# Head squares added on POOL, layer-norm products in rounded parts, and another order of the steps

## The reference, cut to what matters

```python
for i in range(6):
    x = attn_layer(shift_tokens(x), Wqkv[i], q_scale[i], k_scale[i], Wo[i]) + x
    x = ffn_layer(shift_tokens(x), ln_g[i], ln_b[i], W1[i], b1[i], W2[i], b2[i]) + x
# attn_layer: 16 heads of 64; q and k are divided by their norm (l2norm), scaled, rotated;
# windows of 32 tokens see themselves and the window before; softmax; @ Wo
# ffn_layer:
mu = x.mean(-1); var = ((x - mu) ** 2).mean(-1)
xn = (x - mu) / sqrt(var + 1e-05) * g + bln
a, gate = split(xn @ W1 + b1); out = a * gelu(gate) @ W2 + b2
```

## Time and profile before

| | us |
|---|---|
| median of 3 runs | 1853.37 |
| lowest and highest | 1852.04, 1864.84 |
| the profiled execution's own time | 1851.59 |
| its span, first to last instruction | 1849.8 |
| PE busy | 1652.6 (89%) |
| DVE busy | 1239.1 (67%) |
| ACT busy | 1137.9 (62%) |
| POOL busy | 1000.0 (54%) |
| mean granted TensorE clock | 0.962 of full |

### The profile page before, as it was taken

How to read it: one execution, slowest core, us unless ns; L and a number is a source line. 1 busy time by engine, 2 the same in 40 slices (tenths; PEclk the granted TensorE clock), 3 DMA queues, 4 the chain that set the end, 5 groups by cost and what they waited for, 6 DMA issues and landing times.

```text
span 1849.8 us, 80254 instructions
## 1 busy us (share of the span) xinstructions
PE 1652.6 (89%) x35760; PEld 1362.8 (74%) x35760; DVE 1239.1 (67%) x1939; ACT 1137.9 (62%) x2113; POOL 1000.0 (54%) x756
## 2 busy tenths in 40 slices
PE   6458999998999999999999999999999989999986
PEld 5246787777777787778777778778777777778775
DVE  6756766765766775676676677677667667677562
ACT  2024766766666676576676666676666666667653
POOL 1025655664654575565475565476556476556441
PEclk9769999999999999999999999999999999999996
DMA  3047666556646657656656664666665665665650
GB/s 104 1 119 188 135 139 155 124 136 176 162 110 143 155 120 186 148 134 139 155 123 162 155 158 116 144 153 170 155 145 118 151 153 120 150 152 126 140 125 24
DMA packets 98441, 252.92 MB, mean 137 GB/s; under 512 B 30000, under 2 KB 36272, under 8 KB 97328
## 3 DMA queue, kind: packets, MB, share of 16 engines
q1 hardware_dynamic: 98096, 247.80, 56.2%
HBM read 44.26 MB, written 2.10 MB: 25 GB/s over the span
## 4 chain that ended last, share of the span: by engine, by line
PE 53%; DVE 14%; SPq 11%; issue 10%; ACT 8%; DMA 3%; POOL 1%; ACTq 0%; POOLq 0%; DVEq 0%
PE ps L355 48%; SPq L305 6%; SPq L316 6%; DVE E L783 4%; PE ps L542 3%; DMA Qtb<-Qtb 3%; DVE UV L722 2%; DVE rs L793 2%; ACT zs L852 2%; ACT E L852 2%; ACT PT L852 1%; DVE Kt L766 1%; ACT sq L852 1%; PE ps L497 1%; ACT Vs L852 1%
## 5 line engine op out<-in xcount | busy, mean ns | idle before, releaser
L722 DVE SCALAR_TENSOR_TENSOR UV<-ps,veca,rope 128x512 f32<-128x512 f32 x768 | 526.8, 744 | 192.3 <-PE ps L355 182.8
L1081 POOL TENSOR_TENSOR Kt<-UV 128x512 f32<-128x512 f32 x192 | 240.9, 1276 | 472.2 <-DVE UV L722 472.1
L852 ACT ACTIVATE sq<-ps 128x512 f32<-128x512 f32 (+1 forms) x400 | 231.7, 580 | 313.3 <-PE ps L355 299.5
L1081 POOL TENSOR_TENSOR Qtb<-UV 128x512 f32<-128x512 f32 x192 | 242.7, 1286 | 118.5 <-DVE UV L722 118.5
L1091 POOL TENSOR_TENSOR E<-E,mx 128x1024 f32<-128x1024 f32 x96 | 182.6, 1902 | 147.0 <-DVE mx L789 147.0
L355 PE MATMUL ps<-xh,wh 128*128 128x256 f32 x768 | 240.9, 314 | 7.1 <-ACT sq L852 4.3
L355 PE MATMUL ps<-xh,wl 128*128 128x256 f32 x768 | 221.7, 289 | 2.8 <-issue 2.8
L355 PE MATMUL ps<-xl,wh 128*128 128x256 f32 x768 | 221.5, 288 | 1.6 <-issue 1.6
L355 PEld LDWEIGHTS ps<-PT,V 64*64 64x64 f32 x12288 | 198.4, 136 | 31.5 <-issue 19.5
L355 PE MATMUL ps<-Kb,Qtb 64*32 64x64 f32 (+1 forms) x12288 | 190.0, 224 | 34.6 <-issue 34.4
L355 PE MATMUL ps<-PT,V 64*64 64x32 f32 x12288 | 215.5, 221 | 1.6 <-ACT PT L852 0.7
(11 more groups left out here) (131 smaller groups left out, 3347.1 us busy)
## 6 DMA issues: line engine op xcount, KB each, us to landing
V<-Vs SPq DMA_DIRECT2D x672, 128.0 KB
Kb<-Kt SPq DMA_DIRECT2D x384, 128.0 KB
Qtb<-Qtb SPq DMA_DIRECT2D x384, 128.0 KB, 2.4
rope<-in_c_rope SPq DMA_DIRECT2D x48, 512.0 KB
raw<-in_Wqkv SPq DMA_DIRECT2D x6, 1536.0 KB, 6.9
V<-Vs SPq DMA_DIRECT2D x96, 64.0 KB
V<-V SPq DMA_DIRECT2D x96, 64.0 KB, 2.0
wo<-in_Wo SPq DMA_DIRECT2D x6, 512.0 KB, 5.4
```

The source lines that it names most:

```text
L722: e.scalar_tensor_tensor(UV[:, p % 2, slot, :].rearrange("p (i t) -> p i t", i=2), ps[:, half, :].rearrange("p (i t) -> p i t", i=2), veca ...
L852: return e.activation(out, in_, f, **kw)
L1081: e.tensor_tensor(dst, u, v, op).then_inc(s["rot_done"], 1)
```

## The change

Three things change.

1. POOL gets a step a_sum: it adds the squares of the second halves onto those of the first. a_norm then multiplies only once per quarter instead of twice.
2. c_mu and c_var each become two F32R products. For c_mu, ACT rounds zs into the high part za[0], POOL subtracts to get the low part za[1] (c_zal). For c_var, ACT writes the square twice, once plain and once rounded, and POOL makes the remainder (c_zql). cen and mean are rounded once in the preamble.
3. The order of the list is another one.

```diff
+SCHEDULE = """b_lnq b_rcq a_vs0 c_xs c_xb a_vs1 a_v0 w_h0 a_mx0 c_zal w_l0 a_sqy0 c_zsq c_wo b_rq a_sqx0 c_zql a_my0 a_v1
+    a_sqy1 c_rs b_s0 a_x0 a_y0 c_mu a_rot0 b_sub0 b_rqt a_halo b_s1 a_sum0 c_var a_x1 a_sqx1 b_exp0 a_y1 b_scale0
+    b_s2 b_max0 b_s3 a_mx1 c_zl a_x2 b_nrm0 c_zh w_h1 a_y2 b_sub1 a_sqy2 a_my1 a_rl a_lnk a_norm0 b_pto0 c_zn
+    b_sum0 a_rot1 c_h0 b_scale1 b_max1 b_pt0 b_nrm1 a_rh b_exp1 a_rck a_mx2 a_my2 a_sqx2 a_rot2 b_sum1 b_pto1
+    c_gelu0 a_kn0 a_xs+1 b_pt1 b_att0 b_oto0 a_sp0 a_rot3 a_sp1 c_hm0 c_gelu1 b_att1 a_x3 c_h1 a_sum1 a_y3 a_sqy3
+    a_kn1 a_mx3 b_pt2 b_pto2 c_hm1 a_sqx3 b_wo a_xh+1 c_h2 a_my3 w_h2 b_att2 c_gelu2 a_xl+1 c_hm2 b_xb b_pto3
+    b_pt3 b_oto1 c_down c_fin w_l2 w_l1 c_wh c_wl b_att3 a_norm1""".split()
...
             def a_norm(m, side):
-                e.wait_ge(s["sq_done"], m * 8 + 4 * side + 4)
+                e.wait_ge(s["sqs_done"], m * 2 + side + 1)
...
-                for half in range(2):
-                    for q in range(HQ):
-                        ins = mm(ps[q * W:(q + 1) * W, NORM, side * T:(side + 1) * T], ind[:, :],
-                                 sq[:, q // 2, half, q % 2 * T:(q % 2 + 1) * T], half == 0, half == 1,
-                                 tile_position=(0, q * W))
+                for q in range(HQ):
+                    ins = mm(ps[q * W:(q + 1) * W, NORM, side * T:(side + 1) * T], ind[:, :],
+                             sq[:, q // 2, 0, q % 2 * T:(q % 2 + 1) * T], tile_position=(0, q * W))
...
             def c_mu(j, _):
-                e.wait_ge(s["z_act"], j * 2 + 2)
-                mm(ps[:, WO, 0:T], cen[:, :], zs[:, :]).then_inc(s["mu_done"], 1)
+                e.wait_ge(s["zal_done"], j + 1)
+                mm(ps[:, WO, 0:T], cen[:, :], za[:, 0, :], True, False)
+                mm(ps[:, WO, 0:T], cen[:, :], za[:, 1, :], False, True).then_inc(s["mu_done"], 1)
             def c_var(j, _):
-                e.wait_ge(s["zsq_done"], j + 1)
-                mm(ps[:, WO, T:2 * T], mean[:, :], zq[:, :]).then_inc(s["var_done"], 1)
+                e.wait_ge(s["zql_done"], j + 1)
+                mm(ps[:, WO, T:2 * T], mean[:, :], za[:, 0, :], True, False)
+                mm(ps[:, WO, T:2 * T], mean[:, :], za[:, 1, :], False, True).then_inc(s["var_done"], 1)
...
@@ ACT, c_xs and c_zsq
+                if j:
+                    e.wait_ge(s["var_done"], j)
+                e.wait_ge(s["z_act"], j * 2 + 2)
+                act(za[:, 0, :], zs[:, :]).then_inc(s["zah_done"], 1)
...
                 act(zq[:, :], ps[:, WO, 0:T], ACT.Square).then_inc(s["zsq_done"], 1)
+                act(za[:, 0, :], ps[:, WO, 0:T], ACT.Square).then_inc(s["zsq_done"], 1)
...
@@ POOL
+            def a_sum(m, side):
+                e.wait_ge(s["sq_done"], m * 8 + 4 * side + 4)
+                e.tensor_tensor(sq[:, :, 0, :], sq[:, :, 0, :], sq[:, :, 1, :], ALU.add).then_inc(s["sqs_done"], 1)
+            def c_zal(j, _):
+                e.wait_ge(s["zah_done"], j + 1)
+                e.tensor_tensor(za[:, 1, :], zs[:, :], za[:, 0, :], ALU.subtract).then_inc(s["zal_done"], 1)
+            def c_zql(j, _):
+                e.wait_ge(s["zsq_done"], j * 2 + 2)
+                e.tensor_tensor(za[:, 1, :], zq[:, :], za[:, 0, :], ALU.subtract).then_inc(s["zql_done"], 1)
```

More of the change, by code:

```diff
@@ L182, in program @@
         sel = sb("sel", [P, HQ, P], F32R)
-        mean = sb("mean", [P, P])
-        cen = sb("cen", [P, P])
+        mean = sb("mean", [P, P], F32R)
+        cen = sb("cen", [P, P], F32R)
+        za = sb("za", [P, 2, T], F32R)
         ln256 = sb("ln256", [P, 1])
@@ L217, in program @@
             tab_in w_in w1_in veca_in wo_in w2_in vecc_in whv_done whk_done whq_done wlv_done wlk_done wlq_done w1h_done w1l_done xa_done xs_done xh_done xl_done
-            vproj_done vs_done v2_in v2_halo k_in q_in proj_done sq_done mul_done rot_done norm_done rc_done ln_done r_done
+            vproj_done vs_done v2_in v2_halo k_in q_in proj_done sq_done sqs_done mul_done rot_done norm_done rc_done ln_done r_done
             rh_done rl_done rkb_done khat_done k_halo rqt_done rq_done s_done e_done m_done sub_done p_done rs_done
-            ri_done pt_done pts_done pn_done o_done ots_done wo_done xb_done cb_done z_act mu_done
+            ri_done pt_done pts_done pn_done o_done ots_done wo_done xb_done cb_done z_act zah_done zal_done zql_done mu_done
             zsq_done var_done zln_done rstd_done zn_done zb_done zh_done zl_done h_done gelu_done hm_done w2_done
@@ L416, in _ @@
             e.wait_ge(s["x1_done"], G1)
-            e.wait_ge(s["sel_done"], 4)
+            e.wait_ge(s["sel_done"], 6)
             def a_v(m, c):
@@ L633, in _ @@
         def _(e):
-            e.memset(mean[:, :], 1.0 / D).then_inc(s["memset_done"], 1)
+            e.memset(zs[:, 0:P], 1.0 / D).then_inc(s["memset_done"], 1)
             e.memset(XA[:, 0:1], 0.0).then_inc(s["memset_done"], 1)
@@ L657, in _ @@
             e.tensor_copy(identb[:, :], ident[:, :]).then_inc(s["sel_done"], 1)
-            e.tensor_scalar(cen[:, :], ident[:, :], -1.0 / D, None, ALU.add).then_inc(s["sel_done"], 1)
+            e.tensor_scalar(zs[:, P:2 * P], ident[:, :], -1.0 / D, None, ALU.add).then_inc(s["sel_done"], 1)
+            e.tensor_copy(mean[:, :], zs[:, 0:P]).then_inc(s["sel_done"], 1)
+            e.wait_ge(s["sel_done"], 4)
+            e.tensor_copy(cen[:, :], zs[:, P:2 * P]).then_inc(s["sel_done"], 1)
             for g in range(G1):
@@ L1100, in b_nrm @@
                 e.tensor_tensor(ev, ev, ri[:, c].unsqueeze(2).broadcast_to([P, H, KEYS]), ALU.mult).then_inc(s["pn_done"], 1)
-            run({"b_nrm": b_nrm, "w_l": w_l, "c_wl": c_wl, "c_zl": c_zl, "a_xl": a_xl, "a_halo": a_halo, "a_rot": a_rot, "a_rl": a_rl, "b_sub": b_sub},
+            run({"b_nrm": b_nrm, "w_l": w_l, "c_wl": c_wl, "c_zl": c_zl, "c_zal": c_zal, "c_zql": c_zql, "a_xl": a_xl, "a_halo": a_halo, "a_rot": a_rot, "a_rl": a_rl, "a_sum": a_sum, "b_sub": b_sub},
                 lambda g: None)
```

## The result

| | before | after |
|---|---|---|
| median, us | 1855.42 (4 runs) | 1963.82 (4 runs) |
| lowest and highest | 1852.04, 1864.84 | 1960.86, 1973.21 |
| span of the profiled execution | 1849.8 | 1962.4 |
| mean granted TensorE clock | 0.962 | 0.912 |

The ratio is 1.0592, with a 95% interval of 1.0547 to 1.0637. The kernel became slower, as forecast, but by 108 us instead of 44, and the time lies above the range (1830 to 1945).

The account below looks back on a forecast made before the run. It took TensorE to bound b_s0 to a_kn1, with transfers and TensorE nearly level in the rest. The new lap, 21.7 + 13.8 + 0.3 = 35.8 us against 34.87, adds 44 us to 1851.6: 1896, range 1830 to 1945.

Parts of the forecast that it names:

- the bound moves: In the lap, the bound goes from TensorE to VectorE and the transfers in series, making it longer despite 78 us less TensorE work.
- part Y: Lap from b_s0's first score matmul to the end of a_kn1 on VectorE: 21.7 us after the change, without stalls.
- the waits: Sign in the profile after: TensorE waits for POOL sq, POOL E and ACT sq, absent before.
- rival D: POOL sets the pace from b_s0 to a_kn1: an a_sum takes 3.3 us instead of 2.4, 1938 us; chance 0.05.
- part X: Lap from a_kn1's end through key and query transfers to the next b_s0: TensorE floor 13.5 us, mean stays 13.8.
- Stalls: TensorE's issue stalls between b_s0 and a_kn1: mostly vanish in its new idle time, 0.3 us a lap kept (bounds 0 and 0.8).
- rival C: TensorE's clock halves at close waits between b_s0 and a_kn1 in every lap: lap 36.8 us, 1942 us; chance 0.12.
- The sum: New lap 21.7 + 13.8 + 0.3 = 35.8 us against 34.87: +44 us in 47 laps, 1896 us.
- The 20.3 of the prediction: Time before from b_s0 to the end of a_kn1 in one lap, 20.3 us, set against 21.1 on average.
- A: TensorE stays the bound, so the lap sheds 1.6 us: 1774 us, milder forms to 1835; chance 0.15.
- B: The loop has moved but stalls are gone and a_sum is cheap: lap 34.9 to 35.1, 1853 to 1862 us; chance 0.21.

Follow-up runs that it names:

- Kernel 2: The order of the kernel after with the operations of the kernel before (no a_sum, c_zal or c_zql): 1984.88 us, 1.0687 of before.
- kernel 5: The kernel before with one step moved, b_s0 ahead of a_x0 and a_y0 on TensorE: 1924.92 us, 1.0376 of before.
- Kernel 4: The kernel after with b_s0 moved behind a_x0 and a_y0: 2024.4 us, 1.088 of before.
- kernel 3: The kernel after with small unused products filling TensorE's waits ahead of a_norm0, b_pt0 and b_pt1: 1911.48 us, 1.0298 of before.
- kernel 9: The kernel before with only the queries' squares added on POOL (a_sum1), their a_norm1 moved behind the next a_v0: 1855.59 us, 0.9972 of before.
- 1: All new operations in the order of before, a_norm0 moved behind a_y2 and a_norm1 behind c_down: 2138.3 us, 1.1533 of before.
- kernel 11: New layer-norm products and queries' sum in a rearranged order of before, small products filling waits at c_mu, b_pt0 and b_pt1: 1920.44 us, 1.0331 of before.
- kernel 6: The kernel before plus a_sum0 and a_sum1 alone, a_norm0 moved behind a_y2 and a_norm1 behind c_down: 2076.52 us, 1.1202 of before.

## Why the prediction was right, and where it was wrong

**Right: the bound moves, and part Y.** "New Y = 2.0 + 19.2 + 0.5 = 21.7": the least Y is 21.71. Its terms hold one by one: the first multiplication starts 864.15 - 862.07 = 2.08 behind b_s0; VectorE is busy for 19.10; 0.53 is left for waits, of which the 0.17 before c_hm0 stands in the row above. Kernel 2 has the same 21.71 with the old operations, and kernel 5 shows that the cause named, b_s0 ahead of a_x0, makes the kernel slower by itself. Kernel 4 shows that putting it back is no cure in the new order, where X has no room for a_x0 and a_y0.

**Right: a_sum, and the waits.** The group in the page:

```profile
L1095 POOL TENSOR_TENSOR sq<-sq 128x1024 f32<-128x1024 f32 x96 | 227.8, 2373 | 2.3 <-ACT sq L856 0.8
```

2.37 us, against the 2.4 taken from wl<-raw,wh; rival D falls with it. The new waits for POOL sq, POOL E and ACT sq are there. c_var waits 0.49 (0.6 walked) in a lap whose Y is the least.

**Right: part X at full clock.** TensorE's floor was worked out as 13.5 and is 13.60, busy for all of it. I expected the transfers to end X as often as before; they did so in 5 places (3.5 us) instead of 18 (16.5 us):

```profile
PE ps L356 <- DMA Qtb<-Qtb: 3.5, 5, 1.3
```

Before it was:

```profile
PE ps L355 <- DMA Qtb<-Qtb: 16.5, 18, 4.4
```

This too is the clock: in kernel 3, with little half clock, the transfers end last in 25 places again:

```profile
PE ps L356 <- DMA Qtb<-Qtb: 18.6, 25, 2.6
```

**Wrong: the step "Stalls", and with it the weight of rival C.** The sum kept 0.3 us a lap for everything beyond the undisturbed loop, arguing that stalls vanish in TensorE's new idle time, and had no term for half clock. Measured, it is 22.57 - 21.71 = 0.86 in Y, and X is 14.80 where the sum has 13.8: 0.56 + 1.00 = 1.56 us a lap too little, 73 us in 47 laps. Kernel 3 splits this:

- *Half clock, 1.02.* Filling three waits took nearly all of it away, and 0.23 in Y and 0.79 in X came back, 52 us in all.
- *Stalls in Y, 0.33.* In kernel 3 Y still is 0.63 above its least, for the 0.3 of the sum. Short stalls do vanish as argued: one of 1.24 us in b_s3 left the Y of its lap at 21.71 (kernel 3, lap of 844.17). Longer ones don't: in the kernel after, 4.76 us in b_s3, after 1.28 in b_s1, made a Y of 25.49 (lap of 751.00).
- *X, 0.21.* It is 14.01 in kernel 3 instead of 13.8. By the 18.6 us in 25 places above, or some 0.4 a lap on top of the floor of 13.60, this is the transfers.

The signs in the profile show the same. The laps are 37.4 on average and not 35.5 to 36.0, TensorE's share is 85% and not 84% or less, and the granted clock is 0.912 against 0.962, which was the sign set for C.

Rival C had the mechanism and even its place, but got a chance of 0.12, since one wait of 0.74 a lap had never brought the clock down; several in a row were another case. Its price of 1.0 a lap came out (1.02), but by luck: it was meant for Y alone and for every lap. Most of it is in X, where TensorE has no idle time to absorb it (+2.76 in the lap of 490.29), and in 35 of 45 laps. It also named the wait for a_sum0 first, which kernel 2 does not have. The idle time of an engine off the bound is not free when it sets that engine's own speed.

The term for stalls before was misread too. The 20.3 of the prediction comes from a lap with a stall in its Y, in a row of TensorE's timeline that it passed over:

```profile
1068.57 0.57 PE L355 MATMUL ps<-Kb,Qtb 64*32 64x64 f32 x35 [0.67 <-issue]
```

The least Y before is 19.89, the mean 21.35. So stalls and the half clock behind them cost 1.46 a lap there, not 0.8, and the undisturbed Y grew by 1.82, not by 1.4.

The Trainium skill (TensorE: Matmul & The Clock Gate, A second HAM failure mode: psum-queue depth-cycling) tells of a kernel that cycles through PSUM banks, in which "the PE micro-idles between MM groups frequently enough that HAM oscillates" between the two levels (HAM is its name for what sets this clock). This case agrees on short idle times and the clock: the waits of 0.49 to 1.13 us above, and 4.92 us of half clock a lap. Its waits are for ACT and POOL; that PSUM banks play a part, no run here shows. The Trainium skill (TensorE: Matmul & The Clock Gate, What's actually happening) puts the ramp to full speed at under 1% of a typical kernel. That holds for a ramp that is paid once; here, where the clock fell again in most laps, 52 us of 1963.82, or 2.7%, came back when the waits were filled.

**Wrong, to the other side: the old lap.** The 34.87 of the earlier trace rows includes the draining of the pipeline: the last two writings of XA are only 22.5 us apart. The inner laps of before are 35.18. I set a new inner lap, 35.8, against it, which makes the loss 0.31 x 47 = 15 us too large.

**How the two add up.** 1896 + 73 - 15 = 1954; the rest up to 1963.82 is in the start, where the first XA comes 10.5 us later, and which the sum left out. More than half of the 10.5 is in the first lap, 39.34 us at a clock of 0.87 against 33.88 at 0.95 before.

**Rivals A and B** are out: the shortest lap is 35.30 and the mean of the untouched ones 35.52, not 33.3 nor 35.1. Of A it is true that work left TensorE, and kernel 9 shows what the queries' part of that gives by itself: nothing that can be measured.

**What stays open.** The new operations cost nothing in the new order (2 against the kernel after: 21 us less with them, hardly clear of noise) and 15% in the old one, with its sums' matmuls moved back (1); the table shows it as half clock and waits for POOL, but not which of the moved steps of 1 did most. Why half clock comes in some laps and not in others with the same waits, I can't tell from these rows.

## What to carry to other kernels

When a change takes work from the busiest engine, follow the loop through every engine and queue: here the next bound was a chain through VectorE and the transfers that a shift of one step by two places had lengthened. When it leaves TensorE with several short waits close together, price the clock too, in the stretch of the waits and in the full stretch behind it. A cheap test for this is to fill the waits with small products: if the half clock and the time both fall, the clock was a cost. If the time stays, look elsewhere, or see whether the fillers hold something up themselves, as in kernel 11, whose untouched laps grew. And read the undisturbed loop from the shortest laps, not from one lap picked out.

## What the runs showed of the hardware

One wait of 0.74 in a lap did the clock no harm before. Five waits of 0.49 to 1.13, none of them long, went with half clock in 35 of 45 laps of the kernel after, and so did the three of 0.89 to 1.41 (and one of 0.19) in kernel 2; in kernel 6 it was 42 laps. With the waits filled by small products it was 5 of 45. Before, all 11 touched laps had an issue stall, and none came without one. And a filler costs little: 30 products of 128x192 in a lap, by their rows 3.0 us of TensorE, left the least Y at 21.71.
